# Edge columns and destinations in one transfer, rings of seven steps, and first lists loaded ahead of the tables in a two-layer graph kernel

## What is computed

```python
def _cgconv(x, src, dst, edge_attr, Wf, bf, Ws, bs, gamma, beta, rmean, rvar):
    z = jnp.concatenate([x[dst], x[src], edge_attr], axis=-1)
    msg = jax.nn.sigmoid(z @ Wf + bf) * jax.nn.softplus(z @ Ws + bs)
    n = x.shape[0]
    summed = jax.ops.segment_sum(msg, dst, num_segments=n)
    cnt = jax.ops.segment_sum(jnp.ones((dst.shape[0],), x.dtype), dst, num_segments=n)
    out = summed / jnp.maximum(cnt, 1.0)[:, None]
    out = (out - rmean) * jax.lax.rsqrt(rvar + BN_EPS) * gamma + beta
    return out + x
# x1 = _cgconv(x, ...); x2 = _cgconv(x1, ...); result = _layernorm(x + x2, axis=-1)
```

## Time and profile before

| | us |
|---|---|
| median of three runs (2269.26 to 2273.01) | 2270.21 |
| the profiled execution | 2270.27 |
| its span, first to last instruction | 2268.5 |
| busy PE / DVE / ACT / POOL | 1578.1 / 1660.3 / 1382.3 / 1609.7 |
| mean granted TensorE clock | 0.798 |

### The profile page before, as it was taken

One profiled execution on the slowest core, in us unless ns is written; L12 is line 12 of the kernel. 1 busy time (PEld: TensorE's weight loads), 2 busy tenths in 40 slices (PEclk: granted clock), 3 DMA queues, 4 the chain that ended last, 5 costly groups with the idle time before them and its releaser, 6 DMA issues. The chain is left out here.

```text
span 2268.5 us, 35513 instructions
## 1 busy us (share of the span) xinstructions
PE 1578.1 (70%) x7507; PEld 1356.8 (60%) x7507; DVE 1660.3 (73%) x3577; ACT 1382.3 (61%) x1690; POOL 1609.7 (71%) x1587
## 2 busy tenths in 40 slices
PE   7567766776777767677577777666677676767773
PEld 6456665665666666566456666655566565656662
DVE  3677777777777777777557777777777776777777
ACT  4466666666666666666426666666666665666664
POOL 3477777777777777777336777777777777777770
PEclk9888888778778787788698777888787877887775
DMA  8676666666666566666486666666665656666652
GB/s 280 206 193 174 173 176 177 171 177 175 174 181 174 170 179 176 172 177 178 122 280 179 184 177 173 176 179 171 174 177 171 181 174 174 182 176 175 176 155 65
DMA packets 266858, 402.90 MB, mean 178 GB/s; under 512 B 81121, under 2 KB 164270, under 8 KB 266671
## 3 DMA queue, kind: packets, MB, share of 16 engines
q0 software_dynamic: 75264, 205.62, 32.8%
q1 hardware_dynamic: 190974, 194.77, 28.9%
q10 hardware_dynamic: 434, 0.81, 0.1%
HBM read 370.94 MB, written 30.04 MB: 177 GB/s over the span
## 5 line engine op out<-in xcount | busy, mean ns | idle before, releaser
L328 POOL DMA_INDIRECT pre<-s_rows,ends x1568 | 1590.4, 1014 | 569.8 <-issue 442.9
L368 PE MATMUL pre_ps<-rhs,lhs 128*128 128x256 f32 x3136 | 1047.2, 492 | 615.3 <-DVE lhs L553 584.8
L368 PEld LDWEIGHTS pre_ps<-rhs,lhs 128*128 128x128 f32 x3136 | 727.7, 243 | 776.7 <-DVE lhs L553 481.8
L568 DVE TENSOR_TENSOR pre<-pre_ps,pre 128x1024 f32<-128x1024 f32 x392 | 479.3, 1223 | 334.1 <-DMA pre<-s_rows,ends 328.9
L426 ACT ACTIVATE pre<-pre 128x512 f32<-128x512 f32 x392 | 247.0, 630 | 778.0 <-DVE pre L568 773.5
L378 PEld LDWEIGHTS sum_ps<-hot,msg 128*128 128x128 f32 x3136 | 526.6, 230 | 52.8 <-DVE msg L580 11.4
L378 PE MATMUL sum_ps<-hot,msg 128*128 128x64 f32 x3136 | 492.3, 305 | 12.2 <-DVE msg L580 12.2
L431 ACT ACTIVATE logs<-pre 128x1024 f32<-128x1024 f32 x392 | 414.4, 1057 | 12.4
L437 ACT ACTIVATE logs<-logs 128x1024 f32<-128x1024 f32 x392 | 414.1, 1056 | 12.4
L553 DVE TENSOR_SCALAR lhs<-dst_b,base_f,part 64x256 f32<-64x256 f32 x784 | 302.2, 430 | 96.2 <-issue 57.4
L573 DVE SCALAR_TENSOR_TENSOR logs<-pre,logs 128x512 f32<-128x512 f32 x392 | 268.6, 685 | 1.7 <-ACT logs L437 1.7
(11 more groups left out here) (58 smaller groups left out, 181.4 us busy)
## 6 DMA issues: line engine op xcount, KB each, us to landing
dst_b<-dst_floats SPq DMA_DIRECT2D x392, 128.0 KB
lhs<-edge_cols SPq DMA_DIRECT2D x392, 128.0 KB
rhs<-d_rows SPq DMA_DIRECT2D x784, 64.0 KB
pre<-s_rows,ends POOLq DMA_INDIRECT x1568, 3.2
s_rows<-pre SPq DMA_DIRECT2D x24, 512.0 KB, 4.2
d_rows<-logs SPq DMA_DIRECT2D x24, 512.0 KB, 5.9
out<-y_out SPq DMA_DIRECT2D x12, 256.0 KB, 2.3
sp_tab<-group_table SPq DMA_DIRECT2D x100, 0.0 KB
```

Source lines behind the costliest of these rows:

```text
L328: nc.gpsimd.indirect_dma_start(pre[:, j, i, 0:F2], None, s_dram, bass.IndirectOffsetOnAxis(ap=ends[:, k, j * TILES + i, 0:1], axis=0)).the ...
L368: ins = nc.tensor.matmul(pre_ps[:, j % 2, i, :], lhs[:, j, i * P:(i + 1) * P], rhs[:, j, i // 2, :], start=True, stop=True)
L568: nc.vector.tensor_tensor(pre[:, j, :, 0:F2], pre_ps[:, j % 2], pre[:, j, :, 0:F2], ALU.add).then_inc(s_pre[j], 1)
```

## The change

1. **One transfer for edges and destinations.** A new input `edge_and_destination_cols` has 64 rows of edge features and 64 equal rows of destinations as int32 bits. A step loads 128 partitions of `lhs` at once; `dst_b`, `dst_floats` and the CAST are gone, and the comparison reads the int32 bits of `lhs` and writes floats over them.
2. **Rings of seven.** `lhs`, `rhs` and `pre` have seven slots in place of four, step 4k+j in slot (4k+j) mod 7. SyncE waits for the product of seven steps back, GpSimd for the softplus of seven steps back. `logs` has two slots in place of four.
3. **Lists ahead.** `ends` of groups 0 to 2 is loaded at the start of the layer, their `base_i` and `sp_tab` after eight of the source stores, the columns of the first four steps before the destination stores. GpSimd starts when the source table is stored and `choice` is set. `wins` is gone; VectorE reads `base_i`.
4. **The opening.** The source table is staged in seven slots, the destination table in five (`logs`, `msg`, `hot`). In layer 1 the node weights come in three parts; `group_table` is written by GpSimd, which clears `sums` after that and not before; the flag's product on TensorE comes after double window 12 in place of 24; ScalarE's square root comes after its copies. The edge weights (`rhs[0:64]`, seven slots, 896 KB in place of 512) are loaded by ScalarE's queue after its copies. The 25 updates of `x_t` in layer 2 move from the opening into the first 25 steps.

```diff
-        lhs = sb("lhs", [P, SLOTS, STEP], F32)
-        dst_b = sb("dst_b", [P, SLOTS, STEP], F32)
-        rhs = sb("rhs", [P, SLOTS, PAIRS, F2], F32)
-        pre = sb("pre", [P, SLOTS, TILES, 3 * F], F32)
-        logs = sb("logs", [P, SLOTS, TILES, F2], F32)
+        lhs = sb("lhs", [P, RING, STEP], F32)
+        rhs = sb("rhs", [P, RING, PAIRS, F2], F32)
+        pre = sb("pre", [P, RING, TILES, 3 * F], F32)
+        logs = sb("logs", [P, 2, TILES, F2], F32)
...
+        def slot(k, j):
+            return (SLOTS * k + j) % RING
...
+            for k in range(EARLY):
+                load_ends(k, k)
+            for c in range(8):
+                sp.wait_ge(s_copied, 2 * c + 2)
+                store_rows(sp, s_dram, s_stage, c, s_out)
+            if first:
+                sp.wait_ge(table_out, 48)
+            bodies = n_bodies(sp)
+            at = sp.value_load(t["choice"][:, 1:2], min_val=0, max_val=GENERAL_AT * ROW)
+            load_table(at)
+            for k in range(EARLY):
+                load_base(at + k * ROW, k)
+            for c in range(8, STORES):
+                sp.wait_ge(s_copied, min(2 * c + 2, DOUBLES))
+                store_rows(sp, s_dram, s_stage, c, s_out)
+            for n in range(SLOTS):
+                load_edges(n, n * STEP)
+            for c in range(STORES):
+                sp.wait_ge(d_added, min(2 * c + 2, DOUBLES))
+                store_rows(sp, d_dram, d_stage, c, d_out)
...
-                    done(sp, s_hot_t, g, j, SLOTS)
+                    done(sp, s_prod, g, j, RING)
                     sp.sem_inc(passed, 1)
-                    sp.dma_start(dst_b[WIN:P, j, :], t["dst_dram"][bass.ds(blk * GROUP + j * STEP, STEP)]
-                                 .rearrange("(a c) -> a c", a=1).to_broadcast([WIN, STEP])).then_inc(dst_in[j], 16)
-                    done(sp, s_prod, g, j, SLOTS)
-                    sp.sem_inc(passed, 1)
-                    sp.dma_start(lhs[0:FE, j, :], d["edge_t"][:, bass.ds(blk * GROUP + j * STEP, STEP)]
-                                 ).then_inc(edge_in[j], 16)
...
+                    if not (isinstance(g, int) and g == 0):
+                        load_edges(slot(k, j), blk * GROUP + j * STEP)
+                    load_rows(slot(k, j), j, bases)
...
                 for j in range(SLOTS):
-                    done(pool, s_soft, g, j, SLOTS)
+                    done(pool, s_soft, g, j, RING)
...
-                    ins = nc.vector.tensor_scalar(lhs[WIN:P, j, cols], dst_b[WIN:P, j, cols],
+                    ins = nc.vector.tensor_scalar(lhs[WIN:P, at, cols], lhs[WIN:P, at, cols].bitcast(I32),
                                                   base_f[WIN:P, k, PAIRS * j + q:PAIRS * j + q + 1],
                                                   t["part"][WIN:P, 0:1], ALU.subtract, ALU.is_equal)
...
-                done(act, s_msg, g, j, SLOTS)
+                done(act, s_msg, g, j, 2)
...
+                step = SLOTS * k + j
+                if not first and isinstance(b, int) and live(0) and step < DOUBLES:
+
+                    cols = slice(step * F2, (step + 1) * F2)
+                    nc.vector.scalar_tensor_tensor(t["x_t"][:, cols], t["x1_t"][:, cols], t["bn_shift"][:, 1:2],
+                                                   t["x_t"][:, cols], ALU.add, ALU.add)
...
-                    v.wait_ge(wins_in, g * 16)
-                    v.sem_inc(passed, 1)
-                    sum_at = load_bases()
-                    v.sem_inc(dve_has, 1)
+                    sum_at = load_bases((k - 1) % BODY)
```

More of the change, by code:

```diff
@@ L37 @@
 BODY = 7
+EARLY = 3
+RING = 7
 EPAD = GROUPS * GROUP
@@ L335, in _ @@
         def _(pe):
-            pe.wait_ge(w_in, 16) if first else None
+            if first:
+                pe.wait_ge(w_src_in, 16)
             half = {0: slice(F2, 2 * F2), 1: slice(0, F2)}
@@ L340, in _ @@
                 at, which = i % DOUBLES, i // DOUBLES
+                if first and i == DOUBLES:
+                    pe.wait_ge(w_in, 32)
                 if first:
@@ L353, in _ @@
                 ins.then_inc(tables_done, 1)
-                if first and i == DOUBLES - 1:
+                if first and i == 12:
                     pe.wait_ge(flagged, 1)
@@ L814 @@
         "xT": given("x_cols", x_t),
-        "dst": given("destinations", dst),
+        "dst_rows": given("destinations", np.stack([dst[p * ECOLS:(p + 1) * ECOLS + 1] for p in range(P)])),
         "pair_ends": given("pair_ends", np.stack([dst[0:EPAD:PAIR], dst[PAIR - 1:EPAD:PAIR]])),
```

244 lines of the change are left out of this document (110 added, 134 removed).

## The result

The changed kernel takes 2237.82 us (median of 4 runs, 2235.6 to 2245.67), the kernel before 2271.61 (4 runs on the same chip, 2269.26 to 2276.36): a ratio of 0.9855, 95% interval 0.9825 to 0.9884, so it is faster by 1.2 to 1.8%. The forecast was 2226, the range 2211 to 2241. The profiled execution took 2235.6 us with a span of 2233.8; against the 2270.27 of before that is 34.7 us, where the sum had 44.2.

The account below looks back on a forecast made before the run. GpSimd's gathers, four a step at 5.28 us, were taken to bound the kernel. Layer 1 gains 11.6 + 15.9 = 27.5, layer 2 0.9 + 15.8 = 16.7: 2270.3 - 44.2 = 2226 us, range 2211 to 2241.

Parts of the forecast that it names:

- Rival A: The forecast itself, 2226 us; with the bounds on when the destination tables land, 2219 to 2235; chance 0.62.
- B: Destination tables come 4 to 6 us later in each layer, from slower DMA or gathers' share: 2236 us; chance 0.14.
- Rival F: Each of layer 2's 25 moved x_t updates holds a gather for 473 ns, 11.8 us: 2238 us; chance 0.03.
- The ring: Seven slots let GpSimd issue 12 more gathers before waiting for softplus: 15.9 us in layer 1, 15.8 in layer 2.
- Rival D: A list or slot still holds GpSimd at four steps; only 11.6 + 0.9 us are left: 2258; chance 0.05.
- The opening of layer 1: Softplus of step 0 ends at 75.1 us, so GpSimd resumes gathers at 75.9 instead of 87.51: 11.6 us gained.
- The stall: GpSimd's wait after gather 28 for softplus of step 0 remains: 4.6 us in layer 1, about 7 in layer 2.
- Rival C: Softplus of step 0 ends before gather 28 in both layers, 54.6 us gained: 2215.7, down to 2210; chance 0.11.
- The opening of layer 2: Softplus of step 0 ends at 1200.0 us, GpSimd resumes at 1200.8 instead of 1201.75: only 0.9 us gained.
- The gathers' own duration: Mean time of GpSimd's gathers stays unchanged; bounds 10 ns either way, 16 us over 1568 gathers.
- Rival E: Gathers grow as VectorE's denser work meets them; 28 ns each uses up the gain, 50 ns gives 2304; chance 0.05.
- The comparison, the merged transfer, the waits: VectorE's int32 comparison, the single transfer for edges and destinations, and the dropped wait for `wins`: nothing each.

## Why the forecast was right, and where its steps were off

The mechanism is the forecast's, but the number owes something to the width of the range. Rival A, the forecast with its bounds, ended at 2235, and 2237.8 is above it; it is the value of rivals B (2236) and F (2238). But B's mechanism didn't come: the tables landed 2.2 us late in layer 1 and 0.9 early in layer 2, not 4 to 6 late in each, and the DMA engines ran at 0.39 MB/us and not 0.34.

*The ring.* 12 gathers a layer, as forecast. Their price, 15.9 and 15.8 us, is the old pace on both sides, so it can't miss by itself; the check on it is the run with rings of four, by which the ring is worth about 30 of the 31.7 us. Rival D is answered by the timeline: 28 gathers in one run, so nothing else held GpSimd at four steps.

*The opening of layer 1.* This step was off by 4.4 of 11.6 us, in three terms.

The first is the landing of the tables, 2.2 us. The term was "some 0.5 MB of source rows (one store in flight)" left at 30.1 us, with the DMA engines at 0.375 MB/us from there. The engines were faster than that (385 to 397 GB/s from 35 to 60 us). But the source rows were not out. SyncE issues the stores, and it now stops between the eighth and the ninth for the choice and the bases: the rows of its queue show nothing after 23.8, then `sp_tab` at 26.02 and `base_i` at 26.54, and the five last source stores from 28.02 to 32.19. That is 2.4 MB instead of 0.5, while the DMA engines moved 6 GB/s from 26 to 28 us and 3 from 28 to 30. With 2.4 MB, 0.39 MB/us and gathers from 43.4 on, the forecast's own sum gives 64.8; the last table store landed at 64.70, where 62.5 was forecast. The 1.5 us for the last landing in that sum has no row behind it.

The second is the way from there to the first product, 6.2 us instead of 4.4. Before the change SyncE had read the entry of `sp_tab` into its registers ahead of the stores. Now the read stands behind them, on the path of every first row:

```profile
L209 SPq TENSOR_LOAD <-sp_tab x288: 267/562/1847, 64.8 to 2123.9; - x144
```

It begins at 64.8 and takes 1.85 us in each layer (267, 562 and 1847 ns are the shortest, the median and the longest read of the line). The sum had 1.2 us for this read and the entry's transfer together; from the landing to the first load of rows 2.7 pass. The third is the way from the product to softplus, 8.6 instead of 8.2. So the product came at 70.89 (66.9), and softplus ended at 79.47 (75.1).

GpSimd's start, 43.36 instead of 36.0, has three terms of its own. The last source store was issued at 31.32 instead of 30.7. It took 9.6 us to land and not 4.2, with the four stores before it, the edge weights and the columns in flight beside it. The median of the two 256 KB stores, one a layer, was 3.6 us before and is 9.3:

```profile
s_rows<-pre SPq DMA_DIRECT2D x2, 256.0 KB, 3.6
```

```profile
s_rows<-pre SPq DMA_DIRECT2D x2, 256.0 KB, 9.3
```

And from its landing to the first gather 2.4 us passed and not "about 1 us to read".

Is the hole the cause, then? For the gathers' start it is about half: with the entry read behind the stores the last of them still takes 7.0 us to land, and the first gather comes 3.1 to 3.7 us earlier of the 7.4 it was late. For the tables it isn't, since they gained 1.1 us only, 0.6 of it the execution's. They wait for the bytes ahead of them: 1.05 MB of edge columns behind them instead of ahead brought 3.2 us (3.9 less the 0.7 above), where its bytes are 2.7 us at 390 GB/s. VectorE's slots for the destination copies came free earlier as well; whether the rest is theirs no run tells apart.

*The stall.* Forecast 4.6 and 7.2 us, measured 1.95 and 1.94, because the late start moved gather 28 from 71.3 to 78.3 in layer 1, and by 6.2 us in layer 2. Two errors met, which is luck: a later start cost nothing as long as gather 28 came before softplus. Rival C, no stall, was therefore near without its gain.

*The opening of layer 2.* Forecast 0.9, measured 0.0: product 75.34 us after the node counts, before 75.30. The tables landed even earlier than forecast, 69.1 us after the node counts (70.0 forecast, 70.8 before), and the 1.85 us of the register read took back the 1.7 gained. The first gather, expected 41.2 us after the node counts, came 47.56 after (before 45.37); the hole is there too, 80 GB/s in 1125 to 1130. The Trainium skill states (DMA: Bandwidth & Descriptors, section "Issuing engines are not separate DMA queues") that transfers of different engines share the same DMA engines and interleave. The trace agrees: from 20 to 25 us SyncE's queue alone moved 382 GB/s, and from 35 to 60 us SyncE's, ScalarE's and GpSimd's together 390. So what is loaded ahead is paid by the tables, as the run with the columns moved shows for SyncE's own.

*The gathers' own duration.* Forecast unchanged, within 10 ns. Measured 4 ns more after the stall, 1017 to 1021 ns in layer 1 and 1013 to 1017 in layer 2: 2.0 and 1.9 us. VectorE's comparison also grew, 430 to 438 ns. More gathers now begin while VectorE is in softplus, message or comparison, 581 where it was 515, and one that begins in the comparison takes no longer than before (1036 ns, before 1047). Why more of them fall there was not settled; int32 is excluded, and so is the ring of seven, since with rings of four the gathers take 1022 and 1020 ns. Rival E's mechanism exists: the two-input comparison made gathers 25 ns longer in its profiled execution and used up the gain, as its 28 ns would. The change only didn't bring it about.

*Rival F*, the moved updates: 11.8 us were its price, and layer 2's pace lost 1.9, as much as layer 1's 2.0, where no such update runs. It fell as a price, though not as a mechanism: the 25 gathers that ran beside an update took 1106 ns in the mean, 89 more than the layer's, which is 2.2 us. The Trainium skill's rule that I weighed there (SBUF — State Buffer, section "Who interferes with whom") bears on all of VectorE's step: by it an instruction of VectorE with two inputs in SBUF contends with one of GpSimd that reads SBUF, and one with at most one SBUF input doesn't unless it runs in a two-port mode. The table above agrees: 946 ns beside the sums and the comparison from PSUM, 1144 beside the two-input comparison, 1152 and 1238 beside softplus and message. Which mode the pointer form ran in, with its 1036, no run shows.

*The comparison, the merged transfer, the waits:* forecast as nothing each, and no run here takes one of them alone. With rings of four all of them, the openings and the slower pace make 3 us together. Which of them brings the slower pace stays open.

The misses, 4.4 (opening 1), 0.9 (opening 2), 3.9 (pace) and 0.3 (tails), make 9.5 us: 44.2 forecast, 34.7 measured. All are on the costly side of the sum. The first three were each within a bound that I gave, and the median of 2237.8 lies near the end of the range. Two figures of the working are off without moving the sum: at 3.97 against 5.28 us VectorE makes up seven steps in 28 of its own, not 23 (it took 18 and 29), and a tenth in the rate makes the tables of layer 1 3.8 us earlier or 5.0 later, not 3.5 and 4.7.

## What to carry to other kernels

When a fast consumer stalls at a ring's depth, count what the ring will hold before the first release: each slot is worth the pace of one item. What is loaded ahead is put on the queue of an engine that does other things; write out that engine's queue line by line, its waits for small reads too (a register read of 1.85 us behind the last store undid the gain of layer 2), and set early loads behind the transfer that something waits for. Before filling an idle stretch of the DMA engines, ask whether what waits is held by that stretch or by slots and order. And where GpSimd's gathers set the pace, count how many of them begin while VectorE reads two inputs from SBUF.

## What the runs showed of the hardware

- Two of the chips are slower by a quarter in this kernel. In the seven runs there every kernel took 2837 to 2880 us, where the others had 2235 to 2272. Instructions last as long (the 128x1024 addition 1217 and 1222 ns, the shortest gathers alike at 0.94 to 0.95 us), but VectorE stands idle 792 to 826 us in some 140 waits before additions to the sums. The mean granted clock was 0.725 to 0.74 against 0.80 to 0.82.
- The engine behind these waits can be told. The additions wait for TensorE's window sums, and in all seven traces every one of the 949 waits of over 1 us that the trace marks "remote" there ends with the rise of a window sum's semaphore. In the seven other traces these semaphores rise a median 14 ns after the recorded end of the matmul that raises them, on the slow chips 3.1 to 3.4 us after; those of VectorE and ScalarE rise a median 8 to 12 ns after, on both. The lateness begins at 48 to 60 us, after GpSimd's gathers have started. The ends of matmuls in a record are modelled, so whether TensorE finishes late or signals late isn't told, and the cause stays open. The changed kernel itself was not run there; those that differ from it in the comparison or the weights alone had ratios of 0.994 to 0.997 to the kernel before, so a gain of this kind depends on the chip.
- A gather of 128 rows takes 946 ns beside an idle VectorE and beside its instructions with one input from SBUF and one from PSUM, and 1030 (one-hot), 1152 (softplus) or 1238 ns (message) in the mean when it begins in one with two inputs from SBUF. The same comparison costs the gathers that begin in it 198 ns with its second input in SBUF and nothing with it in PSUM, at 485 and 487 ns of its own.
- A read of a table entry into SyncE's registers took 1.85 us right behind the last table store, and a 256 KB store 9.3 us to land in a full queue against 3.6.
- Edge columns of 1.05 MB put behind 6.5 MB of stores instead of ahead brought their end 3.2 us forward, where its bytes alone are 2.7 us.
